# Second context attention: row-group maxima, 32-column values and separate denominators

## What is computed

```python
# 32 query heads, 8 key/value heads, head width 32, 4 query heads per key head
q = (layernorm(x) @ Wq)            # 256 tokens
k, v = ctx @ Wk, ctx @ Wv          # 4096 rows
scores = einsum('bhqd,bhkd->bhqk', q, k) * 32 ** -0.5
probs = softmax(scores, axis=-1)
x = x + (einsum('bhqk,bhkd->bhqd', probs, v) -> heads joined) @ Wo
```

## Time and profile before

| | |
|---|---|
| runs, median (lowest to highest) | 2255.72 us (2251.92 to 2257.29), 3 runs |
| profiled execution, its own time | 2258.47 us |
| its span in the trace | 2257.0 us |
| TensorE busy | 2052.8 us (91%) |
| VectorE busy | 1370.9 us (61%) |
| ScalarE busy | 843.4 us (37%) |
| GpSimd busy | 244.4 us (11%) |
| granted TensorE clock, mean | 0.957 |

### The profile page before, as it was taken

The page is one execution under the profiler, slowest core; times in us unless marked ns, Lnnn a source line. Parts: engine busy times, 40 slices in busy tenths (PEclk is TensorE's granted clock), DMA queues, the critical chain, the costliest instruction groups (busy, mean ns, idle before and its releaser), DMA issues.

```text
span 2257.0 us, 27306 instructions
## 1 busy us (share of the span) xinstructions
PE 2052.8 (91%) x10908; PEld 1502.6 (67%) x10908; DVE 1370.9 (61%) x2070; ACT 843.4 (37%) x1169; POOL 244.4 (11%) x131
## 2 busy tenths in 40 slices
PE   7899999999979999999989767999999999978978
PEld 5799999999968787877778644433333333356843
DVE  3454454454447878797666466666676667266455
ACT  2111111111126666656535212444434443735421
POOL 0000000000006555544000010000000000010000
PEclk9999999999989999999999878999999999989889
DMA  5443343342257656655443161011101110026042
GB/s 178 157 123 117 100 123 117 100 123 79 82 155 212 198 189 200 216 187 178 122 156 120 47 223 38 1 28 29 28 1 28 29 22 7 19 80 245 12 159 86
DMA packets 127869, 243.43 MB, mean 108 GB/s; under 512 B 16525, under 2 KB 79361, under 8 KB 120449
## 3 DMA queue, kind: packets, MB, share of 16 engines
q1 hardware_dynamic: 127745, 241.71, 34.5%
HBM read 177.70 MB, written 63.86 MB: 107 GB/s over the span
## 4 chain that ended last, share of the span: by engine, by line
PE 80%; DVE 11%; DMA 4%; ACT 3%; issue 2%; SPq 0%; POOL 0%; DVEq 0%; ACTq 0%
PE psum L1668 10%; PE psum L467 10%; PE psum L1636 7%; PE psum L1654 4%; PE psum L448 4%; PE psum L450 4%; PE psum L449 3%; PE psum L435 3%; PE psum L277 3%; PE psum L279 3%; PE psum L278 3%; DVE top L1794 3%; PE psum L812 3%; PE psum L814 2%; PE psum L813 2%; PE psum L827 2%
## 5 line engine op out<-in xcount | busy, mean ns | idle before, releaser
L1794 DVE TENSOR_REDUCE top<-psum 128x1 f32<-128x512 f32 x512 | 338.9, 688 | 142.6 <-PE psum L1636 140.8
L1735 ACT ACTIVATE probs_f<-psum 128x1024 f32<-128x1024 f32 x256 | 255.1, 1023 | 308.4 <-PE psum L1654 308.0
L600 DVE TENSOR_REDUCE top<-psum 128x2 f32<-128x512 f32 x272 | 186.5, 691 | 198.1 <-PE psum L435 197.9
L1636 PE MATMUL psum<-k_rows,q_rows 96*128 96x512 f32 x512 | 233.6, 484 | 50.1 <-DMA k_rows<-k_low 22.2
L1668 PE MATMUL psum<-probs_f,v_all 128*64 128x512 f32 x1024 | 274.0, 629 | 0.0
L1636 PEld LDWEIGHTS psum<-k_rows,q_rows 96*128 96x128 f32 x512 | 94.9, 197 | 232.1 <-DVE top L1794 179.3
L903 DVE TENSOR_TENSOR probs_low<-probs,probs_high 128x1024 fp32r<-128x1024 f32 x136 | 194.1, 1432 | 76.8 <-ACT probs L866 76.6
L865 ACT ACTIVATE probs_high<-psum 128x1024 fp32r<-128x1024 f32 x136 | 139.9, 1028 | 161.2 <-PE psum L814 148.3
L448 PE MATMUL psum<-c_high,w_high 128*128 128x256 f32 (+1 forms) x672 | 190.7, 284 | 3.2 <-issue 3.2
L449 PE MATMUL psum<-c_low,w_high 128*128 128x256 f32 (+1 forms) x672 | 190.6, 284 | 0.0
L450 PE MATMUL psum<-c_high,w_low 128*128 128x256 f32 (+1 forms) x672 | 190.5, 284 | 0.0
(11 more groups left out here) (356 smaller groups left out, 3701.3 us busy)
## 6 DMA issues: line engine op xcount, KB each, us to landing
wf_rows<-in_ffn_w_dram SPq DMA_DIRECT2D x42, 512.0 KB, 4.2
staged<-in_ctxT_dram SPq DMA_DIRECT2D x32, 512.0 KB, 5.1
wf_rows<-in_ffn_w_dram SPq DMA_DIRECT2D x8, 1376.0 KB, 7.6
q_dram<-wf_turned SPq DMA_DIRECT2D x42, 256.0 KB, 2.3
gate_up<-q_dram SPq DMA_DIRECT2D x10, 1024.0 KB, 8.1
value_high<-v_high SPq DMA_DIRECT2D x32, 256.0 KB, 3.7
value_low<-v_low SPq DMA_DIRECT2D x32, 256.0 KB, 4.6
k_rows<-k_high SPq DMA_DIRECT2D x16, 512.0 KB, 6.9
```

The lines of the kernel that those rows point to most:

```text
L600: dve.tensor_reduce(top0[:, r0:r0 + 2, n], psum[:, bank, :].rearrange("p (i n) -> p i n", i=2), AX_X, ALU.max).then_inc(*b.bank_read.up())
L1636: pe.matmul(psum[:, bank, :], q_rows[0:3 * HD1, kv, rows * P:(rows + 1) * P], k_rows[kv % 2][0:3 * HD1, chunk * BANK:(chunk + 1) * BANK], ...
L1735: act.activation(probs[n % 4][:], psum[:, 2 * (n % 2):2 * (n % 2) + 2, :].rearrange("p b n -> p (b n)"), ACT.Exp, scale=scale).then_inc(*f ...
L1794: dve.tensor_reduce(top1[:, rows, chunk:chunk + 1], psum[:, 6 + m % 2, :], AX_X, ALU.max).then_inc(*f.max_read.up())
```

## The change

- **Maxima.** The stationary operand is now 32 rows, the rounded query alone (`q_nat_high`); the low parts leave the maxima. The four query heads lie at partitions 0, 32, 64 and 96, and so do four copies of the head's keys (`k_four`, four pieces of 1024 keys, each loaded four times). One *quad* is four matmuls of 32x128 by 512 keys, one to each of banks 4 to 7, and one VectorE reduction of 128x4x512. There are 16 quads a head, one a pair (two at pairs 4 and 8), after the second score block; a quad waits for the reduction of the one before. The negated maxima are one rounded row.
- **Scores.** 97 rows; the two halves go to banks 0 and 1 only, and ACT makes one exponential of 128x512 a bank (four a pair). `q_rows` is filled by 12 loads a head from `q_nat_high` and `q_nat_low`.
- **Values.** The stationary operand is 32 columns; the four products of a pair (two tiles, two halves) go to partitions 0, 32, 64 and 96 of bank 2. `v_pair` holds two heads of values and is loaded in four parts; the ones are gone from `v1_dram`.
- **Denominators.** GpSimd adds the two tiles of a pair (`added`, 126 times); TensorE multiplies ones of 32 columns with two such sums, four matmuls of 256 columns a pair, into bank 3. The last two pairs are summed straight from `probs`.
- **Loads.** The first copies, keys and values are issued at the start of `lora_stage`, ahead of weight panels 27 and 28; `lora_stage` uses `probs` for its tiles.

The diff, cut to its core:

```diff
+        def sp_load_four(kv, piece):
+            rows, at = slice(kv * HD1, (kv + 1) * HD1), slice(piece * REP, (piece + 1) * REP)
+            if kv:
+                sp.wait_ge(*second.max_made.at(16 * (kv - 1) + 4 * (piece + 1)))
+            for g in range(G1):
+                sp.dma_start(k_four[piece][g * HD1:(g + 1) * HD1, :].bitcast(F32),
+                             k1_high[rows, at]).then_inc(*rep_in[piece].up(16))
...
                 sp.dma_start(rank[:], a["rank"]).then_inc(*lora.rank_in.up(16))
+                for piece in range(CTX // REP):
+                    sp_load_four(0, piece)
+                sp_load_keys(0)
+                sp_load_values(0)
                 sp_panel(27)
...
+            def quads_by(pair):
+                return min(QUADS * KV1, pair + QUADS + 2 + (pair >= 4) + (pair >= 8))
...
+                def maxima():
...
+                    if quads:
+                        pe.wait_ge(*f.max_read.at(quads))
+                    for g in range(G1):
+                        rows = slice(g * HD1, (g + 1) * HD1)
+                        done = pe.matmul(psum[:, MAXIMA + g, :], q_nat_high[rows, kv, t * P:(t + 1) * P],
+                                         k_four[piece][rows, at:at + BANK], start=True, stop=True)
+                    done.then_inc(*f.max_made.up())
...
                     for half in range(2):
-                        done = pe.matmul(psum[:, 2 * (n % 2) + half, :], k_rows[kv % 2][:, sn * P:(sn + 1) * P],
-                                         q_rows[:, kv, half * BANK:(half + 1) * BANK], start=True, stop=True)
-                    done.then_inc(*f.scored.up())
+                        block = 2 * n + half
+                        if block >= 2:
+                            pe.wait_ge(*f.exped.at(block - 1))
+                        pe.matmul(psum[:, half, :], k_rows[kv % 2][:, sn * P:(sn + 1) * P],
+                                  q_rows[kv % 2][:, half * BANK:(half + 1) * BANK], start=True,
+                                  stop=True).then_inc(*f.scored.up())
...
+                def weigh(pair):
...
+                    for e in range(2):
+                        value = v_pair[kv // 2 % 2][:, 2 * p + e, kv % 2 * HD1:(kv % 2 + 1) * HD1]
+                        for half in range(2):
+                            row = (2 * e + half) * HD1
+                            done = pe.matmul(psum[row:row + HD1, PRODUCTS, :], value,
+                                             probs[:, (2 * pair + e) % 6, half * BANK:(half + 1) * BANK],
+                                             start=p == 0, stop=p == PER - 1)
...
+                def sum_up(n, part):
...
+                    for e in range(2):
+                        for half in range(2):
+                            row = (2 * e + half) * HD1
+                            done = pe.matmul(psum[row:row + HD1, SUMS, at:at + T], ones[:],
+                                             added[(2 * n + e) % 4][:, half * BANK + at:half * BANK + at + T],
+                                             start=first and part == 0, stop=last,
+                                             skip_group_check=True)
...
                 for pair in range(PAIRS):
+                    kv, p = divmod(pair, PER)
+                    if pair + 1 < PAIRS:
+                        scores(2 * pair + 2)
+                    weigh(pair)
+                    if pair + 1 < PAIRS:
+                        scores(2 * pair + 3)
+                    if p == 13 and kv + 1 < KV1:
+                        turn_tops(kv + 1)
+                    while quads < quads_by(pair):
+                        maxima()
+                    if pair >= 2:
+                        sum_up(pair // 2 - 1, pair % 2)
+                sum_tiles(PAIRS - 2)
+                sum_tiles(PAIRS - 1)
...
-                    dve.tensor_reduce(top1[:, rows, chunk:chunk + 1], psum[:, 6 + m % 2, :], AX_X,
+                    dve.tensor_reduce(top1[:, :, t, chunk], psum[:, MAXIMA:MAXIMA + G1, :], AX_X,
                                       ALU.max).then_inc(*f.max_read.up())
...
+                for pair in range(PAIRS - 2):
+                    n = 2 * pair
+                    pool.wait_ge(*f.exped.at(4 * pair + 4))
+                    if pair >= 4:
+                        pool.wait_ge(*f.summed.at(2 * ((pair - 4) // 2) + 2))
+                    pool.tensor_tensor(added[pair % 4][:], probs[:, n % 6, :], probs[:, (n + 1) % 6, :],
+                                       ALU.add).then_inc(*f.added.up())
```

More of the change, by code:

```diff
@@ new lines, in sum_up @@
+                def sum_up(n, part):
+                    first, last = n % (PER // 2) == 0, n % (PER // 2) == PER // 2 - 1
+                    at = part * T
+                    if part == 0:
+                        pe.wait_ge(*f.added.at(2 * n + 2))
+                    if first and part == 0 and n:
+                        pe.wait_ge(*f.sums_read.at(n // (PER // 2)))
+                    for e in range(2):
[5 more added lines that the diff above has]
+                                             skip_group_check=True)
+                    done.then_inc(*f.summed.up())
@@ new lines, in sum_tiles @@
+                def sum_tiles(pair):
+                    pe.wait_ge(*f.exped.at(4 * pair + 4))
+                    for e in range(2):
+                        for half in range(2):
+                            row = (2 * e + half) * HD1
+                            done = pe.matmul(psum[row:row + HD1, SUMS, :], ones[:],
+                                             probs[:, (2 * pair + e) % 6, half * BANK:(half + 1) * BANK],
+                                             start=False, stop=pair == PAIRS - 1, skip_group_check=True)
+                    done.then_inc(*f.summed.up())
@@ L1781, in scalar_program @@
                         unit += 1
+                upper(KV1 - 1, SUMS)
                 outputs(KV1 - 1, 0)
@@ L1803, in place_low @@
[L1803 to L1814 removed]
+                quads = 0
@@ L1849, in vector_program @@
-                while m < JOBS:
-                    maximum(0, m)
-                    m += 1
-                place_maxima(0)
-                place_low(0)
+                    for _ in range(2 if kv else 0):
+                        maxima()
+                    dve.wait_ge(*f.q_high_set.at(kv + 1))
+                    dve.tensor_tensor(q_nat_low[:, kv, :], psum[:, kv % 4, 0:T], q_nat_high[:, kv, :].bitcast(F32),
+                                      ALU.subtract).then_inc(*f.q_low_set.up())
@@ L1854, in vector_program @@
+                while quads < QUADS + 1:
+                    maxima()
                 unit = WO1
                 for pair in range(PAIRS):
-                    n = 2 * pair
-                    kv, sn = divmod(n, NS1)
-                    more = kv + 1 < KV1
-                    for i in range(4 if n + 2 < 2 * PAIRS else 2):
-                        if more:
-                            for m in beside(sn // 2, i):
-                                maximum(kv + 1, m)
-                        if i >= 2 and sn == NS1 - 2:
-                            take_sum(kv, i - 2)
-                        elif i == 2 and more and sn // 2 == last_pair + 1:
-                            place_low(kv + 1)
@@ L1876, in vector_program @@
+                    if kv and p == 2:
+                        total(kv - 1, SUMS, f.sums_read)
+                    while quads < quads_by(pair):
+                        maxima()
+                    if kv and p in (3, 4):
+                        normalise(kv - 1, p - 3)
+                    if kv and p in (5, 6):
+                        outputs_low(kv - 1, p - 5)
                     if pair >= ahead_from and unit < WO1 + 2:
```

384 lines of the change are left out of this document (181 added, 203 removed).

## The result

| | before | after |
|---|---|---|
| median (lowest to highest) | 2256.51 us (4 runs) | 2171.74 us (2171.48 to 2187.57), 4 runs |
| profiled execution: time, span | 2258.47, 2257.0 | 2171.91, 2170.6 |
| first score | 1393.6 | 1382.8 |
| first score to last values (after: to the closing denominators) | 586.5 | 509.6 |
| from there to the end | 276.9 | 278.2 |

The ratio is 0.9645, interval 0.9599 to 0.969: faster, by 85 us where 96 were forecast. The loop gave 76.9 us (94.8 forecast), its start 10.8 (1 forecast), and the end took 1.3.

A forecast was written before the change was run, and what follows sets the result against it. Bound: TensorE and VectorE ping-pong through two banks with maxima, TensorE alone without. TensorE's terms 464.7 us plus stalls 27 make a 492 us loop, saving 94.8, start 1 sooner: 2160 us, range 2105 to 2232.

The forecast's parts named there:

- Scores, values, denominators: TensorE's pair in the loop: scores 1.34 us as two blocks of 0.67, values 1.01, denominators 0.58.
- rival 3: Values and denominators: four column groups share two streams, 164 us more, 2324 us; chance 0.06.
- Quad: Maxima on TensorE: four matmuls in four row groups take 0.80 us, between bounds 0.44 and 1.13; 111 in the loop.
- rival 1: Maxima: loads into different row groups overlap, so the quad takes 0.44 us, time 2120 us; chance 0.20.
- Stops: Loop stalls, 27 us together: VectorE's division at pairs 3 and 4, turned maxima at pair 13, two banks handed over.
- Pair 13: Loop: next quad waits for turned maxima to be copied out of bank 4 behind two exponentials, 1.1 us, seven times.
- Clock at 1.00 in the loop: Predicted sign in the changed profile: TensorE's granted clock stays at 1.00 throughout the loop.
- The last head: Loop's head without maxima: a pair takes 2.93 us on TensorE.
- The start: Before the loop: projection ends near 1376, row of maxima 17 us later, loop starts at 1393, 1 us sooner.
- Rival 2: Loop: GpSimd's additions become the bound, at the upper bound 4.38 us each, time 2229 us; chance 0.13.
- Rival 4: TensorE's clock: 32-wide groups might lower it to 1.2 GHz, streaming doubles, 2440 us; chance 0.03.
- Rival 5: Quad's cycle through four banks with VectorE's work paces the pair near today's, 4.8 us, no change; chance 0.03.

The follow-up runs named there:

- Experiment 7: Changed kernel with values and denominators in two column groups of 32 instead of four, a pair's two tiles added in the same columns: 2267.02 us, ratio 1.0059.
- experiment 6: Changed kernel with all four matmuls of a quad in one row group, maxima of three of four query heads left out: 2260.72 us, ratio 1.0033.
- Experiment 1: Changed kernel without GpSimd's additions, denominator matmuls reading one tile's exponentials, so denominators miss terms: 2139.30 us, ratio 0.951.
- experiment 8: Changed kernel with half an addition more per pair on GpSimd, into a tile nobody reads: 2190.31 us, ratio 0.9699.
- experiment 5: On top of experiment 4: one more quad ahead of the loop, and denominators before the quad at pair 13: 2114.58 us, ratio 0.9376.
- experiment 3: Changed kernel with the division's multiplications moved to GpSimd between its additions, subtractions two pairs later: 2131.96 us, ratio 0.9465.
- experiment 4: On top of experiment 3: the division's transposes spread over pairs 3 to 6, multiplications and subtractions moved later: 2127.17 us, ratio 0.945.
- experiment 2: Changed kernel without GpSimd's additions, TensorE summing the exponentials itself with 512 columns a tile, denominators right: 2175.72 us, ratio 0.9666.

## Why the prediction was right, and where it wasn't

The change and its direction were foreseen, and the time lay 12 us from the forecast. That it came so near is luck: two of the terms were wrong by 40 and 59 us, with opposite signs, and the start gave 10 us more than it was to. With the quad right and the stops as forecast, it would have been 2120.

- **Scores, values, denominators: right.** 0.67, 0.99 and 0.57 us for 0.67, 1.01 and 0.58. Experiment 7 shows that the gain comes from the four column groups, so rival 3 is out: four share nothing that two did not.
- **Quad: mis-sized.** "I read 0.12 as the step of the loads. Four loads in a row [...] give 0.80, which I take." It measured 0.44, the lower bound: rival 1 was true. In the trace the four loads start 3 to 4 ns apart; in experiment 6, in one row group, 0.11 to 0.24 us. The row read for the step was of loads into the same rows. The price is 0.36 x 111 = 40 us. The Trainium skill ("TensorE: Matmul & The Clock Gate", Measured speedup vs the span model) was nearer: its 3.07 made an estimated 0.51 us, still above the 0.44 of this trace.
- **Stops: the step that failed.** "VectorE divides between two reductions, 0.70 + 0.24 + 0.70 + 2 x 0.41 = 2.5 us [...] about 1.9 us in each of six heads." The 0.41 came from a kernel in which GpSimd did nothing. Beside an addition one of the two took up to 2.61 us. With 27 us for all stops, 86 were lost. Experiment 1 shows the part that the additions cause: some 32 us of the total time, 35 of its loop. The sum itself also counts one division a head where it names two, which at 1.9 us is 11 us more; experiment 1 has 2.4 us a head for VectorE's own part of both. And no term stands for the first head, whose double quads at pairs 4 and 8 and the slow values behind them take about 9 us. The Trainium skill ("SBUF — State Buffer", SBUF: two separate sides) has a VectorE instruction with two SBUF inputs and a GpSimd instruction that reads SBUF exclude each other for their whole length. This trace agrees, with 0.28 us from the end of the one to the end of the other. The prediction did not use it; it asked of GpSimd only whether it was fast enough.
- **Pair 13.** 1.1 us were named, for the right cause; the wait is 1.25, and with the clock behind it 3.0 a head (5.1 + 4.5 for 2 x 3.33). In experiment 1 the same wait costs 1.4 (4.76 + 3.32) where the clock stays. No term stood for clock lost behind a stop. "Clock at 1.00 in the loop" was wrong: 0.91.
- **Net of the loop:** clean pairs 424 us for 465 forecast, stops and lost clock 86 for 27: 510 for 492.
- **The last head** took 3.18 us a pair instead of 2.93, since the second score matmul of a block waits for ACT's exponential; 4 us in all, part of the 424.
- **The start** came 10.8 us sooner instead of 1: the projection ended at 1370 instead of 1376, and the row of maxima took 12.7 us from there instead of 17. The queue's timeline:

```profile
1370.05 0.83 SPq L248 DMA_DIRECT2D panel<-in_wo_dram  x2
...
1370.93 6.04 SPq L1513 DMA_DIRECT2D k_four<-k_high  x8
...
1378.59 0.76 SPq L1963 DMA_DIRECT2D q_rows<-t_high  x1
```

  The order was as forecast (the row behind two panels and eight copies), but 3 MB cleared it sooner than one panel's 5.0 us three times over: panels and copies overlapped, the last of them landing at 1382.67, and the row was issued as soon as its data was there (1378.3 + 0.27).
- **Rival 2** did not come true: an addition takes 2.38 us, near the 2.5 taken and far from the rival's 4.38. That GpSimd can set the pace experiment 8's last head shows, but at 3.70 us an addition and a half, and it is TensorE that waits for it, not ScalarE. **Rival 4** came halfway true by another mechanism: not narrow groups lower the clock (0.97 in experiment 5 with all of them, 1.00 in one of its heads), but stops. **Rival 5** is refuted by the steady pair.

Open: how much of the 41 us of slower running belongs to which stop, and when a short wait costs clock. The wait of 1.25 us at pair 13 was followed within 2 us by the lower level in all six heads of the changed kernel, but in one of six in experiments 1 and 3, in three in experiment 4 and in none in 2 and 7. The wait alone doesn't decide it; no run here isolates what does.

## What to carry over

Before giving GpSimd work beside a busy VectorE, list VectorE's instructions with two SBUF operands that can fall into it, and price each with GpSimd's whole instruction, not with its own. Move such instructions to GpSimd itself, in order between its own, or to where GpSimd pauses; here that and a spread division were worth some 45 us, half as much again as the change had brought (experiment 4), and the work moved around pair 13 and the first head's quads another 13. And when a stop in a dense TensorE stretch is removed, count what it took of the clock afterwards too: over this loop about as much again as the waits (41 us for 45).

## What the hardware showed that was not expected

- Four fp32r matmuls of 32 rows and 512 columns in four row groups take 0.44 us with their loads and the change of shape; in one row group 1.11.
- A VectorE multiplication of 32x256 goes from 0.41 to up to 2.61 us beside a GpSimd addition of 2.38. GpSimd itself needs 0.74 for it.
- Every wait of 1.8 to 3.1 us for a reduction in the changed kernel's loop was followed by the lower clock or ended in it; a wait of 1.25 us was followed by it in all six heads there (values of 1.94 us for 1.06, granted clock 0.76 over 7 us), and in none of six in experiments 2 and 7.
